# An adaLN-style FFN layer on one core: half-sized moves of h, a seventh two-matmul tile of the second layer, and work re-placed on three engines

## Chip, cores, metric

One core of one Trainium2 chip. The metric is the device time of one execution in microseconds (us); lower is better. The kernel before was run three times.

## What is computed

```python
pooled = conditional_pool(x)          # per batch: tanh(x @ W1 + b1) @ v -> scores; masked softmax; p @ x / count
h  = (pooled - mean) * rsqrt(var + eps) * gamma + beta      # over D = 512
y  = silu(h @ dequant(fc1_q, fc1_scales) + fc1_bias)        # 512 -> 2048
z  = y @ dequant(fc2_q, fc2_scales) + fc2_bias              # 2048 -> 512
out = x + (pooled + 0.5 * z)          # x is (16, 512, 512), float32
```

The scales go with groups of 128 rows of a weight, and the inputs are float32.

## The kernel before, in words

There is no scheduler: each engine has its own program, written out by hand, and semaphores join them. There are 16 batches of 512 rows. `ffn(b, p)` is one batch on each engine, and it has `SLOTS` = 32 slots. In slot i TensorE (PE) does four matmuls of the first layer (`fc1`, L1182 and L1183: two tiles, high and low part of h), then what `PE_PLAN` puts there for a later batch, then half of tile k = i // 2 of the second layer (`fc2`, two of the four banks `z_ps`). First-layer work runs five slots ahead of the second (`fc1_slot`), so slots 27 to 31 already do the first tiles of the next batch, b + 1, and need its h, one 128-column chunk c for each of slots 27 to 30.

`fc2` takes three matmuls for a bank and a tile: y_hi by w_hi (L1210), y_hi by w_lo (L1212), y_lo by w_hi (L1213). The tiles in `WHOLE` (0, 3, 5, 9, 10, 11) keep weights that are exact in the high part, and leave L1212 out; the price is that VectorE (DVE) multiplies each of the four banks in PSUM by a ratio (`rescale_z`, L972) before PE goes on to tile k + 1 in it.

ScalarE (ACT) rescales the first layer's partial sums (`rescale`, L658), applies silu (L652), and casts tile k of y to y_hi (`copy`, L571). VectorE makes y_lo = y_f - y_hi (`split_y`, L963), which `fc2` of tile k waits for.

Around this, `ACT_PLAN`, `DVE_PLAN` and `PE_PLAN` place the pooling of batch b + 1 (and, from slot 28 on, the turning of x for batch b + 2). The piece that matters here is the way of h:

- slots 12 to 15: PE makes the four pooled row blocks (`PZ`), ACT scales them into `scratch` (L632), DVE takes their statistics (`LN`, L899), GpSimd (POOL) adds them to x (`residual`, L493), later the bias (`bias`, L501).
- slot 16: DVE computes the reciprocal deviation (`RSTD`) and normalises the four blocks in place in `scratch` (`H`, L919). That posts `h_ready`.
- the sync engine (SP) then turns h in 32 x 32 blocks: `move_h` issues 16 DMAs from `scratch` to `h_cols` (L442), each 32 partitions by 16 blocks. Before it on SP's queue stand eight loads of turned x for the next but one batch (`load_columns`, L376), behind it eight more. Batches 0 and 1 are turned by PE instead, so 14 batches are moved.
- slot 24 (`DVE_MOVED`): DVE transposes inside the blocks, all four chunks c (`TURNH`, L926), and waits for all 16 DMAs first. ACT applies gamma and beta to each chunk in slots 24 to 27 (`AFFINE`, L642), and DVE splits each into hT_hi and hT_lo in slots 25 to 28 (`SPLITH`, L936 and L938). On ACT the order in a slot is rescale (or silu), then AFFINE, then the copy to y_hi.
- slot 28: DVE turns x of batch b + 2 (`TURN` 0 and 1, L805), ACT copies it (`XT` 0, L571), then casts y_hi of tile 15.

Of the kernel before, what the change touches and what calls it, by code (L numbers as in the profile page):

```python
# [5 lines left out]
ALU = mybir.AluOpType  # L6
# [6 lines left out]
P = 128  # L13
Q = 32
# [4 lines left out]
def build(nc, x, itok, cond_w, cond_b, cond_v, gamma, beta, fc1_q, fc1_s, fc1_b, fc2_q, fc2_s, fc2_b, out):  # L19
    B, S, D = x.shape  # L20
    F = fc1_q.shape[1]
    NJ = S // P
    ND = D // P
    NF = F // P
    UNITS1 = ((0, 2), (2, 3), (3, 4), (4, 6), (6, 8), (8, 10), (10, 12), (12, 16))
    UNITS2 = ((0, 1), (1, 2), (2, 3), (3, 4), (4, 5), (5, 6), (6, 8), (8, 9), (9, 12), (12, 16))
    WHOLE = (0, 3, 5, 9, 10, 11)
    EARLY = 3
    SEGMENTS = ((1, 3, 3), (4, 5, 5), (6, 9, 9))
    NZ = NJ * len(WHOLE)  # L30
    NROWS = 2 * ND + NF + 2 + ND * NF
    NG = NF // ND
# [11 lines left out]
    with ExitStack() as ctx:  # L44
# [3 lines left out]
        def sem(name):  # L48
            return ctx.enter_context(nc.semaphore(name))
# [9 lines left out]
        e1 = [sb(f"e1_{i}", [P, ND, NG * P]) for i in range(2)]  # L59
# [114 lines left out]
        def bank(name):  # L174
# [26 lines left out]
        xt_tr = sem("xt_tr")  # L201
        cols_in = [sem(f"cols_in{s}") for s in range(ND)]
        turned = sem("turned")
        h_moved = sem("h_moved")
        h_turned = sem("h_turned")
        xt_hi = sem("xt_hi")
        xt_ready = sem("xt_ready")
# [64 lines left out]
        ACT_TURN = {24: [("HF", 0)], 25: [("HF", 1)], 26: [("HF", 2)], 27: [("HF", 3)]}  # L272
        DVE_TURN = {25: [("SPLITH", 0)], 26: [("SPLITH", 1)], 27: [("SPLITH", 2)], 28: [("SPLITH", 3)]}
        ACT_MOVED = {24: [("AFFINE", 0)], 25: [("AFFINE", 1)], 26: [("AFFINE", 2)], 27: [("AFFINE", 3)]}
        DVE_MOVED = {24: [("TURNH", 0), ("TURNH", 1), ("TURNH", 2), ("TURNH", 3)], 25: [("SPLITH", 0)], 26: [("SPLITH", 1)],
                     27: [("SPLITH", 2)], 28: [("SPLITH", 3)]}
        DELAY = 4

        PE_FIRST = [("USUM", 0), ("U", 0), ("DSUM", 0), ("PZ", 0), ("PZ", 1), ("PZ", 2), ("PZ", 3)]
        ACT_FIRST = [("XT", 0), ("XT", 1), ("XT", 2), ("XT", 3), ("XSH", 0), ("TANH", 0), ("XSH", 1), ("TANH", 1),  # L280
# [5 lines left out]


        DVE_LATE = {0: [("L2", 1), ("D1", 4)], 1: [("D2", 2)], 2: [("D2", 3)], 3: [("L2", 2), ("D1", 6)], 4: [("D2", 4)],
                    5: [("D2", 5)], 6: [("L2", 4)], 7: [("D1", 8)], 8: [("D2", 6)], 10: [("L2", 6)], 11: [("D1", 10)], 12: [("D2", 8)],
                    14: [("L2", 8)], 15: [("D1", 12)], 16: [("D2", 9)], 19: [("D2", 12)], 22: [("L2", 12)]}  # L290
# [71 lines left out]
        def _(sp):  # L362
# [108 lines left out]
        def _(pool):  # L471
# [17 lines left out]
            assert done[0] == POOL_CONSTS  # L489

            def residual(a, p, J):
                pool.wait_ge(pooled_done, a * NJ + (J + 1))
                nc.gpsimd.tensor_tensor(xt[p][:, J, :], xt[p][:, J, :], pooled[J], ALU.add).then_inc(res_added, 1)  # L493

            def bias(a, p, J):
                pool.wait_ge(res_added, a * NJ + (J + 1))
                if J == 0 and is_first(a):
                    pool.wait_ge(hT_done, ND)
                elif J == 0:
                    pool.wait_ge(h_ready, a * NJ + NJ)  # L500
# [62 lines left out]
        def _(act):  # L563
# [109 lines left out]
            def ffn(b):  # L673
                for i in range(SLOTS):
                    ahead, k, c = fc1_slot(i)
                    if not (ahead and is_last(b)):
                        for t in (k, k + 1):
                            if c < ND - 1:
                                rescale(b + ahead, t, c)
                            else:  # L680
                                silu(b + ahead, t)
                        if c == ND - 1:
                            y_hi_part(b + ahead, k)
                    for ahead, name, n in cond_steps(b, i, ACT_PLAN, ACT_TURN, ACT_MOVED):
                        steps[name](b + ahead, n)
                    if i % 4 == 0:
# [33 lines left out]
        def _(dve):  # L720
# [206 lines left out]

            def split_h(a, c, p=None, ch=None):
# [112 lines left out]
        def _(pe):  # L1041
# [258 lines left out]
```

## Time and profile before

| | us |
|---|---|
| median of 3 runs | 1327.86 (1325.63 to 1328.93) |
| the profiled execution | 1327.16 |
| its span, first to last instruction | 1325.4 |
| busy in the span: PE / DVE / ACT / POOL | 1290.2 / 1069.8 / 1009.2 / 201.5 |

The profile is of one execution. The clock granted to TensorE is 1.00 of full from 60 us on. From one batch's first move of h to the next one's it is about 79 us. A time such as 516.98 is us from the start of the span. Matmuls overlap: a row shows 0.39 for one, but they follow each other at 0.23. Rows on SP are the issuing of a DMA, not its transfer.

### The profile page before, as it was taken

What the parts mean: (1) busy time and instruction counts of PE and PEld (TensorE: products, weight loads), DVE (VectorE), ACT (ScalarE), POOL (GpSimd) and SP (SyncE); (2) the same over time, 40 slices, a digit from 0 to 9 for tenths busy, and PEclk for the clock granted to TensorE, in tenths of its full rate; (3) what the DMA queues carried; (4) which work ended last, traced back from release to release, by engine and by line L of the source; (5) the groups of instructions that cost most, each with busy time, mean ns of one, the idle gap of its engine ahead of it and who ended that gap; (6) DMA issues with size and microseconds to landing.
All of it is one profiled execution on the core that took longest, in us unless ns stands there. A gap on an engine that the chain in (4) does not pass through costs nothing.

```text
span 1325.4 us, 20199 instructions
## 1 busy us (share of the span) xinstructions
PE 1290.2 (97%) x5851; PEld 992.9 (75%) x5851; DVE 1069.8 (81%) x2063; ACT 1009.2 (76%) x1661; POOL 201.5 (15%) x166
## 2 busy tenths in 40 slices
PE   7888999999999999999999999999999999999998
PEld 5665877777777777777777777777777777777787
DVE  6999888888788788888888788888878888888744
ACT  3676777877787887778877788877787877778775
POOL 3302111030301203011030301203021020301100
PEclk7999999999999999999999999999999999999999
DMA  7962103131140322213131230313213031230100
GB/s 226 229 217 32 65 15 66 49 64 65 29 101 1 64 65 49 81 17 66 47 64 66 35 94 1 65 66 57 72 19 80 32 64 65 38 90 1 33 32 32
DMA packets 274235, 84.54 MB, mean 64 GB/s; under 512 B 250026, under 2 KB 250692, under 8 KB 273604
## 3 DMA queue, kind: packets, MB, share of 16 engines
q1 hardware_dynamic: 272944, 82.96, 26.4%
q8 instruction: 64, 1.05, 0.3%
q14 instruction: 55, 0.45, 0.1%
q10 hardware_dynamic: 1172, 0.08, 0.1%
HBM read 51.47 MB, written 16.86 MB: 52 GB/s over the span
## 4 chain that ended last, share of the span: by engine, by line
PE 73%; DVE 13%; ACT 6%; issue 4%; SPq 2%; DMA 1%; ACTq 0%; DVEq 0%
PE y_ps L1182 14%; PE z_ps L1210 14%; PE y_ps L1183 13%; PE z_ps L1213 13%; PE z_ps L1212 8%; SPq L442 2%; DVE scratch L919 2%; ACT y_ps L658 2%; ACT L603 1%; DVE z_ps L972 1%; PE a_ps L1141 1%; PE a_ps L1092 1%; DVE y_lo L963 1%; PE a_ps L1093 1%; PE a_ps L1094 1%
## 5 line engine op out<-in xcount | busy, mean ns | idle before, releaser
L658 ACT ACTIVATE y_ps<-y_ps,ratio 128x512 f32<-128x512 f32 x768 | 474.1, 657 | 153.9 <-PE y_ps L1183 152.1
L1210 PE MATMUL z_ps<-w_hi,y_hi 128*128 128x512 f32 x1024 | 414.0, 404 | 11.4 <-DVE z_ps L972 7.4
L1182 PE MATMUL y_ps<-hT_hi,w 128*128 128x512 f32 x1016 | 409.2, 403 | 7.7 <-ACT y_ps L658 5.3
L1213 PE MATMUL z_ps<-w_hi,y_lo 128*128 128x512 f32 x1024 | 400.8, 391 | 0.0
L1183 PE MATMUL y_ps<-hT_lo,w 128*128 128x512 f32 x1016 | 397.5, 391 | 0.0
L963 DVE TENSOR_TENSOR y_lo<-y_f,y_hi 128x512 fp32r<-128x512 f32 x256 | 198.8, 777 | 146.1 <-ACT y_hi L571 144.9
L1210 PEld LDWEIGHTS z_ps<-w_hi,y_hi 128*128 128x128 f32 x1024 | 192.7, 188 | 84.9 <-issue 25.6
L1182 PEld LDWEIGHTS y_ps<-hT_hi,w 128*128 128x128 f32 x1016 | 191.1, 188 | 86.3 <-ACT y_ps L658 33.4
L1212 PE MATMUL z_ps<-w_lo,y_hi 128*128 128x512 f32 x640 | 249.8, 390 | 0.0
L652 ACT ACTIVATE y_f<-y_ps,vec_cols,mant 128x512 f32<-128x512 f32 x256 | 185.1, 775 | 73.8 <-PE y_ps L1183 73.4
L493 POOL TENSOR_TENSOR x<-x,scratch 128x512 f32<-128x512 f32 x64 | 91.6, 1434 | 941.6 <-ACT scratch L632 941.6
L1213 PEld LDWEIGHTS z_ps<-w_hi,y_lo 128*128 128x128 f32 x1024 | 192.9, 188 | 39.7 <-issue 0.2
L1183 PEld LDWEIGHTS y_ps<-hT_lo,w 128*128 128x128 f32 x1016 | 191.6, 189 | 34.5
L571 ACT ACTIVATE y_hi<-y_f 128x512 fp32r<-128x512 f32 x256 | 160.4, 626 | 1.3 <-PE z_ps L1213 1.3
L1212 PEld LDWEIGHTS z_ps<-w_lo,y_hi 128*128 128x128 f32 x640 | 120.2, 188 | 26.8 <-issue 3.4
L972 DVE TENSOR_TENSOR z_ps<-z_ps,z_ratio 128x512 f32<-128x512 f32 x192 | 122.3, 690 | 0.5
L972 DVE TENSOR_TENSOR z_ps<-z_ps,e 128x512 f32<-128x512 f32 x192 | 119.4, 688 | 0.0
L501 POOL TENSOR_TENSOR x<-x,b2h 128x512 f32<-128x512 f32 x64 | 96.0, 1528 | 82.5 <-DVE scratch L919 73.1
L899 DVE BATCH_NORM_STATS2 stats<-scratch 128x6 f32<-128x512 f32 x64 | 44.0, 688 | 26.4 <-ACT scratch L632 26.4
L632 ACT ACTIVATE scratch<-a_ps,columns 128x512 f32<-128x512 f32 x64 | 44.1, 688 | 22.6 <-DVE columns L891 18.4
L642 ACT ACTIVATE h_rows<-h_rows,vec_cols 128x512 f32<-128x512 f32 x56 | 45.7, 817 | 13.3 <-DVE h_rows L926 13.3
L817 DVE TENSOR_TENSOR xs_lo<-x,xs_hi 128x512 fp32r<-128x512 f32 x60 | 41.6, 693 | 2.1
(207 smaller groups left out, 1166.3 us busy)
## 6 DMA issues: line engine op xcount, KB each, us to landing
x<-in_x_dram SPq DMA_DIRECT2D x64, 256.0 KB, 3.2
out_dram<-x SPq DMA_DIRECT2D x64, 256.0 KB, 2.7
x_cols<-in_x_dram SPq DMA_DIRECT2D x240, 64.0 KB, 2.2
h_cols<-scratch SPq DMA_DIRECT2D x224, 64.0 KB, 2.1
fc_codes<-in_L_ffn_fc_q_dram SPq DMA_DIRECT2D x8, 1024.0 KB, 12.5
fc_scaled<-units_dram SPq DMA_DIRECT2D x4, 1024.0 KB, 17.8
e<-powers_dram SPq DMA_DIRECT2D x3, 1024.0 KB, 15.6
h_rows<-powers_dram SPq DMA_DIRECT2D x1, 1024.0 KB, 10.8
```

Of the source, the lines that this page charges most:

```text
L493: nc.gpsimd.tensor_tensor(xt[p][:, J, :], xt[p][:, J, :], pooled[J], ALU.add).then_inc(res_added, 1)
L501: nc.gpsimd.tensor_tensor(xt[p][:, J, :], xt[p][:, J, :], b2h[:], ALU.add).then_inc(bias_added, 1)
L571: return nc.scalar.activation(o, i, ACT.Copy)
L652: nc.scalar.activation(y_f[k % 2][:], y_ps[k % 2][:], ACT.Silu, bias=b1[:, k:k + 1], scale=mant[:, (ND - 1) * NF + k:(ND - 1) * NF + k + 1 ...
L658: nc.scalar.activation(y_ps[k % 2][:], y_ps[k % 2][:], ACT.Copy, scale=ratio[:, c * NF + k:c * NF + k + 1]).then_inc(scaled, 1)
L963: v.tensor_tensor(y_lo[k % 2][:], y_f[k % 2][:], f32(y_hi[k % 2][:]), ALU.subtract).then_inc(split_done, 1)
L972: v.tensor_tensor(z_ps[r][:], z_ps[r][:], z_ratios[WHOLE.index(k)], ALU.mult).then_inc(z_scaled, 1)
L1182: mm(o, w, hT_hi[:, c, :], start=(c == 0), stop=False, skip_group_check=True)
L1183: last = mm(o, w, hT_lo[:, c, :], start=False, stop=True, skip_group_check=True)
L1210: mm(z_ps[r][:], y_hi[k % 2][:, rows], w2_hi[:, k, :], start=(k == 0), stop=False, skip_group_check=True)
L1212: mm(z_ps[r][:], y_hi[k % 2][:, rows], w2_lo[:, k, :], start=False, stop=False, skip_group_check=True)
L1213: last = mm(z_ps[r][:], y_lo[k % 2][:, rows], w2_hi[:, k, :], start=False, stop=(k == NF - 1 or k in WHOLE), skip_group_check=True)
```

## The change

1. `WHOLE` gets tile 7 (two matmuls for a bank and a tile instead of three, and four more rescales on DVE, in slots 15 and 16).
2. H writes to `normal`, a view of `e1[0]`, a weight-loading buffer that is free by then, laid out as two halves of 256 columns. `move_h` moves each half by itself: 2 x 16 DMAs of 32 partitions by 8 blocks, each half with its own semaphore. TURNH 0 and 1 stay in slot 24 and wait for the first half; TURNH 2 goes to slot 25, behind SPLITH 0, and TURNH 3 to slot 26, behind SPLITH 1; they wait for the second half.
3. POOL's `residual` waits for all of H (h_ready) and H no longer waits for it; `bias` waits for hT_done.
4. The cast of tile 5 to y_hi goes from ACT to DVE (`cast_y`, slot 9); the split of tile 9 goes from slot 17 to slot 16, ahead of H.

```diff
-    UNITS2 = (..., (5, 6), (6, 8), (8, 9), (9, 12), (12, 16))
-    WHOLE = (0, 3, 5, 9, 10, 11)
+    UNITS2 = (..., (5, 6), (6, 7), (7, 8), (8, 9), (9, 12), (12, 16))
+    WHOLE = (0, 3, 5, 7, 9, 10, 11)
...
-        DVE_MOVED = {24: [("TURNH", 0), ("TURNH", 1), ("TURNH", 2), ("TURNH", 3)], 25: [("SPLITH", 0)], 26: [("SPLITH", 1)],
+        DVE_MOVED = {24: [("TURNH", 0), ("TURNH", 1)], 25: [("SPLITH", 0), ("TURNH", 2)], 26: [("SPLITH", 1), ("TURNH", 3)],
                      27: [("SPLITH", 2)], 28: [("SPLITH", 3)]}
+        Y_CAST = 5
+        Y_SOON = 9
+        normal = e1[0][:].rearrange("p j d -> p (j d)").rearrange("p (h j d) -> p h j d", h=2, j=NJ)
...
             def move_h(a):
-                rows = scratch[:, 0:NJ * D].rearrange("p (n d) -> p n d", d=P)
                 sp.wait_ge(h_ready, a * NJ + NJ)
-                for i in range(P // Q):
-                    for j in range(P // Q):
-                        piece = slice(j * Q, (j + 1) * Q)
-                        sp.dma_start(h_cols[piece, :, i * Q:(i + 1) * Q], rows[i * Q:(i + 1) * Q, :, piece]).then_inc(h_moved, 16)
+                for half in range(2):
+                    blocks = slice(half * 2 * NJ, (half + 1) * 2 * NJ)
+                    rows = normal[:, half, :, :].rearrange("p j (c d) -> p (j c) d", d=P)
+                    for i in range(P // Q):
+                        for j in range(P // Q):
+                            piece = slice(j * Q, (j + 1) * Q)
+                            sp.dma_start(h_cols[piece, blocks, i * Q:(i + 1) * Q],
+                                         rows[i * Q:(i + 1) * Q, :, piece]).then_inc(h_moved[half], 16)
...
             def residual(a, p, J):
-                pool.wait_ge(pooled_done, a * NJ + (J + 1))
+                if is_first(a):
+                    pool.wait_ge(pooled_done, J + 1)
+                elif J == 0:
+                    pool.wait_ge(h_ready, a * NJ + NJ)
...
             def turn_h(a, c, p, ch):
-                if c == 0:
-                    dve.wait_ge(h_moved, (a - 1) * 256)
-                chunk = h_cols[:].rearrange("p (j c) n -> p j c n", j=NJ)[:, :, c, :]
+                if c % 2 == 0:
+                    dve.wait_ge(h_moved[c // 2], (a - 1) * 256)
+                chunk = h_cols[:].rearrange("p (h j c) n -> p h j c n", h=2, j=NJ)[:, c // 2, :, c % 2, :]
```

**VectorE, slots 15 and 16 of a batch.** y_lo0 is tile 8, y_lo1 tile 9; L899 and L913 are the statistics of row blocks 2 and 3, L919 and L935 are H. Before:

```order
L963 TENSOR_TENSOR y_lo0<-y_f0,y_hi0 128x512
L899 BN_STATS stats<-scratch 128x6 x2
L903 MEMSET columns4 128x4
...
L919 TENSOR_SCALAR scratch<-scratch,mv,columns4 128x512 x4
L963 TENSOR_TENSOR y_lo1<-y_f1,y_hi1 128x512
```

After:

```order
L979 TENSOR_TENSOR y_lo0<-y_f0,y_hi0 128x512
L993 TENSOR_TENSOR z_ps0<-z_ps0,e1_1 128x512
L993 TENSOR_TENSOR z_ps1<-z_ps1,e1_1 128x512
L913 BN_STATS stats<-scratch 128x6
L993 TENSOR_TENSOR z_ps2<-z_ps2,e1_1 128x512
L993 TENSOR_TENSOR z_ps3<-z_ps3,e1_1 128x512
L913 BN_STATS stats<-scratch 128x6
L917 MEMSET columns4 128x4
...
L979 TENSOR_TENSOR y_lo1<-y_f1,y_hi1 128x512
L935 TENSOR_SCALAR e1_0<-scratch,mv,columns4 128x2x256 x4
```

Four rescales now stand ahead of the last statistics, and y_lo of tile 9 ahead of H.

**The sync engine, one batch, moves of h** (x_cols are the loads of turned x). Before, and after:

```order
L442 DMA h_cols<-scratch 32x16x32 [waits h_ready]
L442 DMA h_cols<-scratch 32x16x32 x15
```

```order
L452 DMA h_cols<-e_0 32x8x32 [waits h_ready]
L452 DMA h_cols<-e_0 32x8x32 x31
```

16 issues of 16 blocks have become 32 issues of 8 blocks.

**VectorE, slots 24 to 28** (L926 and L942 are TURNH; L936/L938 and L952/L954 SPLITH; y_lo1 is tile 13, y_lo0 tile 14). Before:

```order
L926 STREAM_TRANSPOSE h_rows<-h_cols 128x512 x4
L963 TENSOR_TENSOR y_lo1<-y_f1,y_hi1 128x512
L936 CAST hT_hi<-h_rows 128x512
L938 TENSOR_TENSOR hT_lo<-h_rows,hT_hi 128x512
L936 CAST hT_hi<-h_rows 128x512
L938 TENSOR_TENSOR hT_lo<-h_rows,hT_hi 128x512
L963 TENSOR_TENSOR y_lo0<-y_f0,y_hi0 128x512
```

After:

```order
L942 STREAM_TRANSPOSE h_rows<-h_cols 128x512 x2
L979 TENSOR_TENSOR y_lo1<-y_f1,y_hi1 128x512
L952 CAST hT_hi<-h_rows 128x512
L954 TENSOR_TENSOR hT_lo<-h_rows,hT_hi 128x512
L942 STREAM_TRANSPOSE h_rows<-h_cols 128x512
L952 CAST hT_hi<-h_rows 128x512
L954 TENSOR_TENSOR hT_lo<-h_rows,hT_hi 128x512
L942 STREAM_TRANSPOSE h_rows<-h_cols 128x512
L979 TENSOR_TENSOR y_lo0<-y_f0,y_hi0 128x512
```

The transposes of chunks 2 and 3, the first of which waits for the second half, now stand between the two splits and ahead of y_lo of tile 14.

## Rows read from the trace of the kernel before

**Rows 1.** The page: busy time by engine, and the chain's shares by engine.

```profile
PE 1290.2 (97%) x5851; PEld 992.9 (75%) x5851; DVE 1069.8 (81%) x2063; ACT 1009.2 (76%) x1661; POOL 201.5 (15%) x166
...
PE 73%; DVE 13%; ACT 6%; issue 4%; SPq 2%; DMA 1%; ACTq 0%; DVEq 0%
```

**Rows 2.** The chain that ended last, in one batch: start us, us, what.

```profile
515.03 1.93 DVE scratch L919 x4
516.98 0.62 SPq L442
...
528.00 2.08 DMA h_cols<-scratch
530.10 0.72 DVE h_rows L926
531.57 0.61 ACT y_hi L571
532.18 0.55 ACT y_ps L658
532.78 0.49 PE y_ps L1182
...
565.66 0.51 ACT y_hi L571
...
596.61 0.61 DVE y_lo L963
597.27 0.50 PE z_ps L1210
```

**Rows 3.** Timeline, PE: start us, us, engine line, tiles; ten matmuls each apart.

```profile
537.57 0.39 PE L1182 MATMUL y_ps<-hT_hi,w 128*128 128x512 f32 x1
...
539.83 0.39 PE L1182 MATMUL y_ps<-hT_hi,w 128*128 128x512 f32 x1
...
542.10 0.44 PE L1182 MATMUL y_ps<-hT_hi,w 128*128 128x512 f32 x1
```

**Rows 4.** Timeline, VectorE, slots 15 to 28; last bracket: idle before and releaser.

```profile
509.11 0.69 DVE L899 BATCH_NORM_STATS2 stats<-scratch 128x6 f32<-128x512 f32 x1
511.51 0.69 DVE L899 BATCH_NORM_STATS2 stats<-scratch 128x6 f32<-128x512 f32 x1 [1.71 <-ACT scratch L632]
...
520.42 2.48 DVE L972 TENSOR_TENSOR z_ps<-z_ps,e 128x512 f32<-128x512 f32 x4
...
530.10 2.49 DVE L926 STREAM_TRANSPOSE h_rows<-h_cols 128x512 f32<-128x512 f32 x4 [0.19 <-DMA h_cols<-scratch]
...
533.08 0.42 DVE L936 CAST hT_hi<-h_rows 128x512 fp32r<-128x512 f32 x1
...
534.14 0.42 DVE L936 CAST hT_hi<-h_rows 128x512 fp32r<-128x512 f32 x1
...
539.55 1.29 DVE L805 STREAM_TRANSPOSE scratch<-x_cols 128x512 f32<-128x512 f32 x2
```

**Rows 5.** Timeline, SP: the issuing of DMAs.

```profile
8.62 0.59 SPq L410 DMA_DIRECT2D powers_dram<-powers  x1
...
17.40 0.69 SPq L414 DMA_DIRECT2D units_dram<-h_rows  x1
...
115.31 8.29 SPq L376 DMA_DIRECT2D x_cols<-in_x_dram  x16
```

**Rows 6.** Timeline, SP: the moves of h in the batch of rows 2, and the last.

```profile
516.98 11.65 SPq L442 DMA_DIRECT2D h_cols<-scratch  x16
...
1229.54 10.71 SPq L442 DMA_DIRECT2D h_cols<-scratch  x16
```

**Rows 7.** Timeline, ACT, slots 28 and 29.

```profile
540.29 0.63 ACT L571 ACTIVATE part_hi<-scratch 128x512 fp32r<-128x512 f32 x1 [0.71 <-DVE scratch L805]
540.83 0.62 ACT L571 ACTIVATE y_hi<-y_f 128x512 fp32r<-128x512 f32 x1
541.35 1.22 ACT L658 ACTIVATE y_ps<-y_ps,ratio 128x512 f32<-128x512 f32 x2
```

**Rows 8.** Stretches: us, busy (count) PE, PEld, DVE, ACT, POOL, clock, DMA share, GB/s.

```profile
52.00:56.00 4.00, 2.36 (x9) 1.18 (x9) 4.00 (x4) 3.08 (x6) 4.00 (x3) 1.00 0.73 113
56.00:60.00 4.00, 4.00 (x12) 3.13 (x11) 4.00 (x7) 3.01 (x6) 0.34 (x1) 0.57 0.89 209
```

More of the change, by code:

```diff
@@ L25, in build @@
     UNITS1 = ((0, 2), (2, 3), (3, 4), (4, 6), (6, 8), (8, 10), (10, 12), (12, 16))
-    UNITS2 = ((0, 1), (1, 2), (2, 3), (3, 4), (4, 5), (5, 6), (6, 8), (8, 9), (9, 12), (12, 16))
-    WHOLE = (0, 3, 5, 9, 10, 11)
+    UNITS2 = ((0, 1), (1, 2), (2, 3), (3, 4), (4, 5), (5, 6), (6, 7), (7, 8), (8, 9), (9, 12), (12, 16))
+    WHOLE = (0, 3, 5, 7, 9, 10, 11)
     EARLY = 3
-    SEGMENTS = ((1, 3, 3), (4, 5, 5), (6, 9, 9))
+    SEGMENTS = ((1, 3, 3), (4, 5, 5), (6, 7, 7), (8, 9, 9))
     NZ = NJ * len(WHOLE)
@@ L203, in build @@
         turned = sem("turned")
-        h_moved = sem("h_moved")
+        h_moved = [sem(f"h_moved{half}") for half in range(2)]
         h_turned = sem("h_turned")
@@ L274, in build @@
         ACT_MOVED = {24: [("AFFINE", 0)], 25: [("AFFINE", 1)], 26: [("AFFINE", 2)], 27: [("AFFINE", 3)]}
-        DVE_MOVED = {24: [("TURNH", 0), ("TURNH", 1), ("TURNH", 2), ("TURNH", 3)], 25: [("SPLITH", 0)], 26: [("SPLITH", 1)],
+        DVE_MOVED = {24: [("TURNH", 0), ("TURNH", 1)], 25: [("SPLITH", 0), ("TURNH", 2)], 26: [("SPLITH", 1), ("TURNH", 3)],
                      27: [("SPLITH", 2)], 28: [("SPLITH", 3)]}
         DELAY = 4
+        Y_CAST = 5
+        Y_SOON = 9
+        Y_AT = 16
         PE_FIRST = [("USUM", 0), ("U", 0), ("DSUM", 0), ("PZ", 0), ("PZ", 1), ("PZ", 2), ("PZ", 3)]
@@ L288, in build @@
         DVE_LATE = {0: [("L2", 1), ("D1", 4)], 1: [("D2", 2)], 2: [("D2", 3)], 3: [("L2", 2), ("D1", 6)], 4: [("D2", 4)],
-                    5: [("D2", 5)], 6: [("L2", 4)], 7: [("D1", 8)], 8: [("D2", 6)], 10: [("L2", 6)], 11: [("D1", 10)], 12: [("D2", 8)],
+                    5: [("D2", 5)], 6: [("L2", 4)], 7: [("D1", 8)], 8: [("D2", 6)], 9: [("D2", 7)], 10: [("L2", 6)], 11: [("D1", 10)], 12: [("D2", 8)],
                     14: [("L2", 8)], 15: [("D1", 12)], 16: [("D2", 9)], 19: [("D2", 12)], 22: [("L2", 12)]}
@@ L344, in xt_buffers, with by_halves @@
             return first_xt(s) if is_first(a) else (xt_rows[s], hi[:], lo[:])
+        normal = e1[0][:].rearrange("p j d -> p (j d)").rearrange("p (h j d) -> p h j d", h=2, j=NJ)
+        def by_halves(ap):
+            return ap.rearrange("p (h d) -> p h d", h=2)
         def w1_views(k0):
@@ L496, in bias @@
                 pool.wait_ge(res_added, a * NJ + (J + 1))
[L497 to L500, printed above, removed]
+                if J == 0:
+                    pool.wait_ge(hT_done, a * ND + ND)
                 nc.gpsimd.tensor_tensor(xt[p][:, J, :], xt[p][:, J, :], b2h[:], ALU.add).then_inc(bias_added, 1)
@@ L685, in ffn @@
                         steps[name](b + ahead, n)
-                    if i % 4 == 0:
+                    if i % 4 == 0 and i // 2 + 1 != Y_CAST:
                         y_hi_part(b, i // 2 + 1)
@@ L801, in turn_columns @@
             def turn_columns(a, s, p, ch):
-                if s == 0 and by_pe(a - 1):
-                    dve.wait_ge(h_tr, a * ND)
+                if s == 0:
+                    dve.wait_ge(res_added, a * NJ)
+                    if by_pe(a - 1):
+                        dve.wait_ge(h_tr, a * ND)
                 dve.wait_ge(cols_in[s], a * 64)
@@ L917, in normalise @@
                 for J in range(NJ):
-                    dve.wait_ge(res_added, a * NJ + (J + 1))
-                    v.tensor_scalar(pooled[J], pooled[J], mv[:, J, 0:1], rstd[1][:, J:J + 1], ALU.subtract,
+                    if is_first(a):
+                        dve.wait_ge(res_added, J + 1)
+                    o, i = (pooled[J], pooled[J]) if is_first(a) else (normal[:, :, J, :], by_halves(pooled[J]))
+                    v.tensor_scalar(o, i, mv[:, J, 0:1], rstd[1][:, J:J + 1], ALU.subtract,
                                     ALU.mult).then_inc(h_ready, 1)
             def turn_h(a, c, p, ch):
-                if c == 0:
-                    dve.wait_ge(h_moved, (a - 1) * 256)
-                chunk = h_cols[:].rearrange("p (j c) n -> p j c n", j=NJ)[:, :, c, :]
+                if c % 2 == 0:
+                    dve.wait_ge(h_moved[c // 2], (a - 1) * 256)
+                chunk = h_cols[:].rearrange("p (h j c) n -> p h j c n", h=2, j=NJ)[:, c // 2, :, c % 2, :]
                 v.transpose(by_block(h_rows[:, c, :]), chunk).then_inc(h_turned, 1)
@@ L963, in split_y, with cast_y @@
                 v.tensor_tensor(y_lo[k % 2][:], y_f[k % 2][:], f32(y_hi[k % 2][:]), ALU.subtract).then_inc(split_done, 1)
+            def cast_y(b, k):
+                dve.wait_ge(silu_done, b * NF + k + 1)
+                dve.wait_ge(fc2_done, b * NF + (k - 1))
+                v.tensor_copy(y_hi[k % 2][:], y_f[k % 2][:]).then_inc(yhi_done, 1)
             def rescale_z(b, k, r):
@@ L986, in ffn @@
                         split_y(b, (i + 1) // 2)
-                    if i % 4 == 1:
+                    if i % 4 == 1 and (i // 2 + 1 != Y_SOON or is_first(b)):
+                        if i // 2 + 1 == Y_CAST:
+                            cast_y(b, Y_CAST)
                         split_y(b, i // 2 + 1)
@@ L997, in ffn @@
                     for ahead, name, n in cond_steps(b, i, DVE_PLAN_FIRST if is_first(b) else DVE_PLAN, DVE_TURN, DVE_MOVED):
+                        if name == "H" and not is_first(b):
+                            split_y(b, Y_SOON)
                         steps[name](b + ahead, n, p if ahead == 2 else 1 - p, chains[ahead])
+                    if is_last(b) and i == Y_AT:
+                        split_y(b, Y_SOON)
                     if is_first(b):
@@ L1160, in transpose_h @@
                 for J in range(NJ):
-                    last = nc.tensor.transpose(a_ps[c % 2][:, J * P:(J + 1) * P], pooled[J][:, c * P:(c + 1) * P], ident[:])
+                    last = nc.tensor.transpose(a_ps[c % 2][:, J * P:(J + 1) * P], normal[:, c // 2, J, (c % 2) * P:(c % 2 + 1) * P], ident[:])
                 last.then_inc(h_tr, 1)
```

## The prediction

> **What bounds the kernel now.** I read the page first. TensorE is busy for 97% of the span and makes 73% of the chain that ended last; no other engine is busy for more than 81% [rows 1]. So a matmul less is worth its own time, wherever nothing else becomes late. What one is worth is read from the timeline of PE: from 537.57 to 539.83 stand ten matmuls of 512 columns, so one follows another at 0.227 us, and 0.39 is only how long each shows [rows 3]. These ten are also one slot, 2.26 us.
>
> Then I read where the chain leaves PE, and in one batch it does so once at length [rows 2]: H on VectorE ends and releases SP at 516.98, SP issues the 16 moves of h, the last of them is issued at 528.00 and lands 2.08 later, TURNH starts at 530.10, and then AFFINE 0, the cast of tile 13 (531.57) and a rescale (532.18) stand one behind the other on ACT until PE goes on at 532.78. VectorE waited only 0.19 for the landing [rows 4]. So the way of h, 13.1 us from the first issue to TURNH, fits before slot 24 with nothing over. A change to it has to be costed on SP, not on PE.
>
> **Tile 7 with two matmuls.** Four matmuls less in a batch: 4 x 0.227 = 0.91 us, in slots 14 and 15. Four rescales more on VectorE: four in a row take 2.48, 0.60 each from start to start [rows 4]. Two fall in the 1.71 us in which VectorE waited at 511.51. Statistics 2 start at 510.3 instead of 509.11, the third and fourth rescale need PE's last matmul of tile 7 (about 510.9) and end at 512.2, and statistics 3 start there instead of at 511.51: H is 0.7 later. PE does not wait for them, since its tile 8 starts at about 512.
>
> **Tile 9 ahead of H.** y_lo of tile 9 took 0.61 behind H, and PE stood for it: its tile 9 began at 597.27, when that was done [rows 2]. Now it is done before; PE gains some 0.4 at that place, and H is another 0.6 later. Together SP starts its moves at 516.98 + 1.3 = 518.3, while PE is 0.9 to 1.3 ahead of where it was.
>
> **Tile 5 cast by VectorE.** The copy on ACT stood in the chain with 0.51 us [rows 2], which is the upper bound of the gain; nothing is the lower one, if another wait ends last there. I take 0.3.
>
> **The moves.** This is the term that decides. One issue shows 11.65 / 16 = 0.73 us [rows 6]; the last series takes 10.71, which is 0.67 for each, and the 0.94 more of this one lies in a single slow issue; I put one such into each batch. What does an issue of half the blocks take? No row shows one. The issue of 512 pieces of 128 bytes takes 0.67. The two other DMAs that read fewer than 128 partitions of on-chip memory took 0.59 with 64 pieces (64 rows of `powers`) and 0.69 with 1408 (64 partitions x 22) [rows 5]. So from 64 to 1408 pieces the issue grows by 0.1, and 256 pieces should take about 0.61, with the 0.04 between two issues 0.65. The bounds: 0.67, if it does not shrink at all, and 0.34, if it is all in the pieces. The loads of turned x, from HBM, have 512 pieces too and 8.29 / 16 = 0.52 [rows 5]; that is a value between. I take 0.65, since its rows are of the same kind of source.
>
> The Trainium skill (DMA: Bandwidth & Descriptors, Anatomy of one DMA) speaks against the change too: it calls the fixed part of a DMA independent of its size, and says that many descriptors can be emitted before their cost shows. By it alone the issue would keep its 0.67.
>
> *First half*: its 16th issue starts at 518.3 + 15 x 0.65 + 0.9 = 528.95 and lands at 531.0, where 530.1 was. TURNH 0 is 0.9 later than before, while PE comes 0.9 to 1.3 earlier. So the wait on ACT's rescale at 532.78 grows, and PE goes on there at about 533.7.
>
> *Second half*: its last issue starts at 518.3 + 31 x 0.65 + 0.9 = 539.4 and lands at 541.5. TURNH 2 is wanted at about 535. VectorE stands until 541.5, and behind it stand TURNH 2 (0.62), SPLITH 1 (1.06, from one CAST to the next), TURNH 3 (0.62), y_lo of tile 14 (0.61), SPLITH 2 and 3 (2.12) and TURN 0 [rows 4]. PE needs SPLITH 1 in slot 28, at 537.57 before [rows 3]; it comes at 543.2. ACT stands in AFFINE 2 over the same time, with the rescale of slot 27 behind it. TURN 0 starts at 546.5, XT 0 on ACT 0.74 later, and behind XT 0 come the cast of tile 15 (0.54), the rescale of slot 29 (0.52), and PE 0.75 after that rescale's start [rows 3, 7]. That is 549.05 where 542.10 stood: 6.95 later. The gains of tiles 7 and 9 are swallowed by this wait, since what follows hangs on SP; tile 5's 0.3 is kept, as it is ahead of the pooling. Net 6.65 us in each of 14 batches, 93 us.
>
> *TensorE's clock.* PE stands idle for nearly 5 us in slot 27 to 28. In the first 60 us it was busy for 2.36 of 4 us in one stretch, and the granted clock of the next was 0.57, that is mostly 1.2 GHz instead of 2.4 [rows 8]. I expect such a fall in each of the 14 batches. A stretch of 4 us at 0.57 loses 4 x 0.43 = 1.7 us; about 1 us of it lies in the wait for the rescale of slot 29. So 0.7 x 14 = 10 us, between 0 and 24.
>
> The Trainium skill (TensorE: Matmul & The Clock Gate, Part 1) says that activity releases the throttle and idling brings it back; no row in the steady batches shows it yet.
>
> **Pool and the rest.** Residuals and bias of a batch are needed at its end, 80 us later. H lost its wait for POOL, which did not end last (H followed the deviation at once). Turned x of chunk 2 is loaded behind 32 issues instead of 16, lands at about 544 and is wanted at about 550. All three cost nothing. If the moves were quick, their cover would still be there.
>
> **Sum.** Two batches (0 and 15) have no moved h in their slots and gain 0.9 + 0.4 + 0.3 = 1.6 each: -3. Then 93 + 10 - 3 = +100 on the profiled execution's 1327.2 gives 1427 us. The profiled execution is within 1 us of the median of the runs shown.
>
> **Rivals.**
> 1. *Issuing goes with the pieces* (faster). An issue takes 0.34 to 0.38 with its gap. Then the second half lands by 533, before TURNH 2 wants it, nothing waits, and all batches keep their 1.6: 1327.2 - 16 x 1.6 = 1302 us. For it: a load shows 0.52 with just as many pieces, so 0.67 is not a floor. Against it: 64 pieces took 0.59. It decides at 0.44 for an issue: the delay of a batch is 31 x issue - 13.5, which is 6.65 at 0.65 and nothing at 0.44. Chance 0.14. The Trainium skill (DMA: Bandwidth & Descriptors, Bandwidth) calls transfers under 64 KB descriptor-dominated; by that sentence the halves of 32 KB would each cost half, and this rival would be the case.
> 2. *Issues of about 0.52*, as the loads of x. 31 x 0.52 - 13.5 = 2.6 for a batch, 14 x 2.6 - 3 = +34: 1361 us, and up to 1375 with some loss of clock. Chance 0.13.
> 3. *The clock stays low for longer* after each wait, and loses all of 1.7 us or somewhat more: 14 x 1.0 to 2.0 on top of the forecast, 1441 to 1455 us. Chance 0.13.
> 4. *VectorE becomes the bound.* It has 2.4 + 0.4 us more in some 79, of which 65 are busy now; it would be at 87%, so only order matters, which is in the sum. Not given a chance of its own.
>
> **How the numbers follow.** Forecast 0.58, rival 3 0.13, rival 2 0.13, rival 1 0.14, and 0.02 that gains and waits just balance. The time is the forecast's, 1427 us. Its own range is 1405 to 1440 (0.63 and 0.67 for an issue, 0 to 1 us for the clock). The range to hold 8 in 10 goes to rival 2 below and through rival 3 above: 1355 to 1462. A difference of 0.3%, 4 us, is about what a measurement of this kernel tells from no change. Faster by more: 0.14. Within: 0.02. Slower by more: 0.84.
>
> **What would show it.** In the profile after: 32 issues a batch on SP in about 21.5 us, not 11 (wrong if below 15); VectorE idle for 5 to 7 us before a STREAM_TRANSPOSE of h_rows, released by the DMA of h_cols, 14 times; an idle of some 5 us before L1182's matmul in slot 28; about 86 us from batch to batch instead of 79; a granted clock below 1.00 in stretches behind these waits; L1212's line with 576 instead of 640 matmuls. The prediction is wrong if TURNH 2 starts without waiting.

## The result, and the profile after

| | before | after |
|---|---|---|
| median, us | 1328.16 (4 runs) | 1439.0 (4 runs, 1431.55 to 1442.16) |
| ratio | 1 | 1.083, 95% interval 1.0786 to 1.0874 |
| span of the profiled execution | 1325.4 | 1436.5 |
| mean granted clock of TensorE | 0.992 | 0.965 |
| from one batch's first move of h to the next one's | 79.2 | 87.2 |

The change makes the kernel 8.3% slower. The two page lines that answer to [rows 1]:

```profile
PE 1306.2 (91%) x5787; PEld 1000.6 (70%) x5787; DVE 1129.2 (79%) x2144; ACT 1005.6 (70%) x1645; POOL 207.0 (14%) x168
...
PE 46%; SPq 19%; DVE 18%; issue 7%; ACT 7%; DMA 2%; ACTq 0%; DVEq 0%
```

There are 64 matmuls less, and PE makes 46% of the chain instead of 73%; SP, which only issues DMAs, makes 19% instead of 2%. The timeline of SP in one batch, to set beside [rows 6], gives the start in us from the start of the span, the duration in us, and what was issued:

```profile
719.12 4.06 SPq L384 DMA_DIRECT2D x_cols<-in_x_dram  x8
726.99 21.50 SPq L452 DMA_DIRECT2D h_cols<-e  x32
748.68 4.18 SPq L384 DMA_DIRECT2D x_cols<-in_x_dram  x8
```

32 issues take 21.5 us. VectorE in the same batch, for [rows 4]:

```profile
720.93 0.68 DVE L913 BATCH_NORM_STATS2 stats<-scratch 128x6 f32<-128x512 f32 x1
...
739.35 1.30 DVE L942 STREAM_TRANSPOSE h_rows<-h_cols 128x512 f32<-128x512 f32 x2 [1.06 <-DMA h_cols<-e]
741.47 0.69 DVE L979 TENSOR_TENSOR y_lo<-y_f,y_hi 128x512 fp32r<-128x512 f32 x1 [0.81 <-ACT y_hi L583]
742.08 0.42 DVE L952 CAST hT_hi<-h_rows 128x512 fp32r<-128x512 f32 x1
742.53 0.69 DVE L954 TENSOR_TENSOR hT_lo<-h_rows,hT_hi 128x512 fp32r<-128x512 f32 x1
749.81 0.71 DVE L942 STREAM_TRANSPOSE h_rows<-h_cols 128x512 f32<-128x512 f32 x1 [6.59 <-DMA h_cols<-e]
...
756.72 1.39 DVE L979 TENSOR_TENSOR y_lo<-y_f,y_hi 128x512 fp32r<-128x512 f32 x1 [0.63 <-ACT y_hi L583]
758.03 1.78 DVE L824 TENSOR_TENSOR part_lo<-scratch,part_hi 128x512 fp32r<-128x512 f32 x1
```

TURNH 0 waits 1.06 us for the first half, and TURNH 2 then waits 6.59 us for the second. The last two lines are slower than they were: y_lo took 0.69 and part_lo, the low part of a chunk of x, 0.68 at this place before, and POOL adds the bias beside them now. Who waits behind the second half, for the whole span (engine, line, for whom: us in total, times, longest):

```profile
PEld y_ps L1209 <- ACT y_ps L670: 117.9, 76, 5.4
DVE h_rows L942 <- DMA h_cols<-e: 107.4, 28, 6.6
ACT h_rows L654 <- DVE h_rows L942: 104.3, 28, 5.4
```

The wait goes from the DMA to VectorE, from there to ACT's AFFINE, and from the rescale that stands behind it on ACT to PE. 28 waits are two in each of the 14 batches with moved h. PE in the same batch, and then the whole core in stretches of 4 us (columns as in [rows 8]):

```profile
751.97 0.79 PE L1209 MATMUL y_ps<-hT_hi,w 128*128 128x512 f32 x1 [4.99 <-ACT y_ps L670]
...
759.87 0.50 PE L1119 MATMUL a_ps<-part_hi,wc_hi 128*128 128x512 f32 x1
```

```profile
744.00:748.00 4.00, 2.98 (x14) 2.13 (x12) 0.00 (x0) 1.14 (x2) 0.00 (x0) 1.00 0.32 53
748.00:752.00 4.00, 0.03 (x1) 0.03 (x1) 2.15 (x4) 1.44 (x3) 0.00 (x0) 0.69 0.54 86
752.00:756.00 4.00, 4.00 (x10) 3.13 (x11) 3.93 (x8) 3.02 (x5) 0.98 (x1) 0.50 0.42 67
756.00:760.00 4.00, 3.90 (x17) 2.88 (x16) 3.37 (x4) 3.04 (x6) 4.00 (x4) 0.95 0.00 0
```

After 4.99 us of idling the granted clock is 0.50, the lower level of 1.2 GHz, for one stretch, in which PE does 10 matmuls instead of some 18. L1119 is PE's first matmul on the next but one batch's x, and it waits for part_lo.

### The profile page after: what moved, and what is told of

The parts are those of the page before. It is cut to its first block, busy times and chain, and to the rows that moved or that the text cites. A ratio compares the mean times of both kernels' runs of the same rounds, so it can differ in the third digit from the quotient of the medians.

```text
span 1436.5 us, 20429 instructions
## 1 busy us (share of the span) xinstructions
PE 1306.2 (91%) x5787; PEld 1000.6 (70%) x5787; DVE 1129.2 (79%) x2144; ACT 1005.6 (70%) x1645; POOL 207.0 (14%) x168
## 4 chain that ended last, share of the span: by engine, by line
PE 46%; SPq 19%; DVE 18%; issue 7%; ACT 7%; DMA 2%; ACTq 0%; DVEq 0%
SPq L452 19%; PE y_ps L1209 9%; PE z_ps L1237 8%; PE y_ps L1210 8%; PE z_ps L1240 8%; PE z_ps L1239 6%; DVE z_ps L993 3%; DVE y_lo L979 3%; ACT y_ps L670 2%; DVE e L935 2%; DMA h_cols<-e 2%; ACT y_hi L583 2%; DVE stats L913 1%; ACT L615 1%; PE a_ps L1119 1%
## 5 line engine op out<-in xcount | busy, mean ns | idle before, releaser
L1209 PE MATMUL y_ps<-hT_hi,w 128*128 128x512 f32 x1016 | 415.1, 409 | 94.2 <-ACT y_ps L670 89.8
L1237 PE MATMUL z_ps<-w_hi,y_hi 128*128 128x512 f32 x1024 | 421.0, 411 | 15.2 <-DVE z_ps L993 13.0
L1210 PE MATMUL y_ps<-hT_lo,w 128*128 128x512 f32 x1016 | 405.1, 399 | 0.0
L1209 PEld LDWEIGHTS y_ps<-hT_hi,w 128*128 128x128 f32 x1016 | 196.1, 193 | 170.1 <-ACT y_ps L670 117.9
L1239 PE MATMUL z_ps<-w_lo,y_hi 128*128 128x512 f32 x576 | 231.5, 402 | 0.0
L507 POOL TENSOR_TENSOR x<-x,scratch 128x512 f32<-128x512 f32 x64 | 97.6, 1555 | 827.5 <-DVE e L935 817.1
L993 DVE TENSOR_TENSOR z_ps<-z_ps,e 128x512 f32<-128x512 f32 x256 | 160.5, 686 | 0.6
L583 ACT ACTIVATE y_hi<-y_f 128x512 fp32r<-128x512 f32 x240 | 150.2, 626 | 1.3 <-PE z_ps L1240 1.3
L1239 PEld LDWEIGHTS z_ps<-w_lo,y_hi 128*128 128x128 f32 x576 | 112.3, 195 | 26.1 <-issue 3.4
L942 DVE STREAM_TRANSPOSE h_rows<-h_cols 128x512 f32<-128x512 f32 x56 | 38.1, 699 | 107.4 <-DMA h_cols<-e 107.4
L913 DVE BATCH_NORM_STATS2 stats<-scratch 128x6 f32<-128x512 f32 x64 | 43.8, 685 | 2.0 <-ACT scratch L644 2.0
```

The source lines that it names most:

```text
L583: return nc.scalar.activation(o, i, ACT.Copy)
L1209: mm(o, w, hT_hi[:, c, :], start=(c == 0), stop=False, skip_group_check=True)
L1210: last = mm(o, w, hT_lo[:, c, :], start=False, stop=True, skip_group_check=True)
L1237: mm(z_ps[r][:], y_hi[k % 2][:, rows], w2_hi[:, k, :], start=(k == 0), stop=False, skip_group_check=True)
L1239: mm(z_ps[r][:], y_hi[k % 2][:, rows], w2_lo[:, k, :], start=False, stop=False, skip_group_check=True)
```

## The experiments

Theory: one issue on SP costs 0.65 us whatever its size, so the doubled moves bring the second half too late. Rivals for the 111 us: the later H, the rescales of the seventh tile, POOL's moved work, the clock. Times are medians. Each group of runs has its own runs of the kernel before, with medians of 1327.7 to 1328.6, and a ratio is always to those.

**The halves alone, and all but the halves.** The first kernel is the changed one with tile 7, tile 5, tile 9 and POOL put back:

```diff
-    WHOLE = (0, 3, 5, 7, 9, 10, 11)
+    WHOLE = (0, 3, 5, 9, 10, 11)
...
-        Y_CAST = 5
-        Y_SOON = 9
+        Y_CAST = -1
+        Y_SOON = -1
...
+                pool.wait_ge(pooled_done, a * NJ + (J + 1))
...
-                    pool.wait_ge(hT_done, a * ND + ND)
+                    pool.wait_ge(*((hT_done, ND) if is_first(a) else (h_ready, a * NJ + NJ)))
```

The last two places are the waits of `residual` and of `bias`.

> The kernel before with the halved buffer and the 32 half moves alone; tile 7 has three matmuls again, tiles 5 and 9 and POOL's work stand where they stood. Theory (an issue costs 0.65 us whatever its size, and the second half lands late): H is not delayed here, so the second half lands at 516.98 + 31 x 0.65 + 0.9 + 2.1 = 540.1 in the old batch's times, PE's slot 30 starts 7.7 later, at 547.8 instead of 542.1: 5.7 us a batch, 80 in all, and the clock falls as well, 10 to 25 us: 1417 to 1432 us, VectorE waiting 5 us for the DMA of h_cols 14 times. Rival (the loss comes from the delayed H, from tile 7's rescales and from POOL's moved work): 1335 us or less.

Measured: 1419.2 us, ratio 1.0685 (1.0653 to 1.0716), as the theory has it. VectorE waited for the DMA 14 times, 6.3 us each, where 5 were expected:

```profile
DVE h_rows L939 <- DMA h_cols<-e: 88.0, 14, 6.6
```

The second keeps all of the change but makes the moves whole again:

```diff
-                for half in range(2):
-                    blocks = slice(half * 2 * NJ, (half + 1) * 2 * NJ)
-                    rows = normal[:, half, :, :].rearrange("p j (c d) -> p (j c) d", d=P)
+                rows = normal.rearrange("p h j (c d) -> p (h j c) d", d=P)
...
-                if c % 2 == 0:
-                    dve.wait_ge(h_moved[c // 2], (a - 1) * 256)
+                if c == 0:
+                    dve.wait_ge(h_moved[0], (a - 1) * 256)
```

> The changed kernel with one DMA for both halves again: 16 moves of 16 blocks from the new buffer, TURNH 0 waits for all of them; everything else as changed. Theory: the 100 us are the 16 more issues. But H starts its moves 1.3 us later than before, and the landing, not PE, sets slot 26: a batch gains only tile 5's 0.3 and loses 1.3 less what VectorE had to spare, so 1327 + 14 x 1.0 - 3 = 1338 us, between 1325 and 1345, clock 1.00 in the steady batches. Rival (POOL's bias beside the splits, or the seventh rescale, cost much of it): 1370 us or more.

Measured: 1363.8 us, ratio 1.026 (1.0238 to 1.0281). Taking the 16 issues away gives back 75 of the 111 us. But 1363.8 is well above 1338 and outside 1325 to 1345, and closer to the rival's 1370 than to the theory: the rest of the change costs 36 us, where I had 11. Its timeline and waits:

```profile
612.51 11.68 SPq L450 DMA_DIRECT2D h_cols<-e  x16
```

```profile
DVE h_rows L940 <- DMA h_cols<-e: 25.2, 14, 2.8
PEld a_ps L1117 <- DVE part_lo L822: 24.1, 15, 1.8
```

The first wait is the late H (0.7 us in two waits before). The second does not occur before at this line, and leads to POOL.

**POOL's bias.** To the kernel above:

```diff
-                    pool.wait_ge(hT_done, a * ND + ND)
+                    pool.wait_ge(*((hT_done, ND) if is_first(a) else (h_ready, a * NJ + NJ)))
```

> As one_move, and POOL's bias waits for H instead of for the splits, as before. In the changed kernel three SBUF operations of VectorE in slots 29 and 30 took 2.3 us longer while POOL added the bias. Theory (POOL beside VectorE delays the copy that PE waits for): 10 to 20 us faster than one_move. Rival (POOL disturbs VectorE as much at its other place, where y_lo took 1.79 instead of 0.69): no difference beyond 4 us.

Measured: 1351.6 us, 12 faster, as the theory has it. In one_move POOL's four additions stood here:

```profile
635.41 5.93 POOL L511 TENSOR_TENSOR x<-x,b2h 128x512 f32<-128x512 f32 x4 [16.87 <-DVE hT_lo L952]
```

and VectorE beside them:

```profile
637.02 1.48 DVE L977 TENSOR_TENSOR y_lo<-y_f,y_hi 128x512 fp32r<-128x512 f32 x1 [0.63 <-ACT y_hi L581]
638.43 1.76 DVE L822 TENSOR_TENSOR part_lo<-scratch,part_hi 128x512 fp32r<-128x512 f32 x1
640.11 0.70 DVE L817 STREAM_TRANSPOSE scratch<-x_cols 128x512 f32<-128x512 f32 x1
640.74 1.15 DVE L822 TENSOR_TENSOR u_rows<-scratch,coef 128x512 fp32r<-128x512 f32 x1
```

Operations that take 0.65 to 0.69 elsewhere take 1.15 to 1.76, and PE's first projection of the batch after next waits for part_lo.

**The clock.** The changed kernel with work of no use in PE's idle time, in batches 1 to 14:

```diff
+                    if i == 27 and not is_first(b) and not is_last(b):
+                        filler.append(b)
...
+                    if filler:
+                        pe.wait_ge(pooled_done, filler.pop() * NJ + 2 * NJ)
+                        for _ in range(20):
+                            mm(a_ps[0][:], wc_hi[:, 0, :], wc_hi[:].rearrange("p c a -> p (c a)"), start=True, stop=True)
```

> The changed kernel with 20 matmuls of no use (512 columns, 4.5 us) at the end of slot 27 of batches 1 to 14, where PE stands idle for 5.4 us. Theory: the wait stays as long, and the clock does not fall, so the batch loses only the wait: 10 to 25 us faster than the changed kernel, 1414 to 1429, clock 0.99. Rival (the slots behind the wait are bound by VectorE and ACT and not by PE's clock): the clock stays up, and the time is that of the changed kernel within 5 us.

Measured: 1440.0 us against 1439.0, ratio to before 1.0845 (1.0822 to 1.0868). The rival holds: the four runs of the changed kernel spread over 10.6 us, so the two medians fix the difference only to some 6 us, but the 10 to 25 us of the theory are not there. PE filled its time and the clock stayed up:

```profile
744.00 4.70 PE L1265 MATMUL a_ps<-wc_hi 128*128 128x512 f32 x20
749.66 0.50 PE L1209 MATMUL y_ps<-hT_hi,w 128*128 128x512 f32 x1 [0.96 <-ACT y_ps L670]
```

```profile
748.00:752.00 4.00, 3.04 (x14) 1.99 (x13) 3.90 (x9) 3.75 (x6) 0.00 (x0) 1.00 0.73 114
752.00:756.00 4.00, 3.65 (x16) 2.44 (x14) 3.37 (x5) 2.81 (x7) 3.28 (x3) 1.00 0.01 3
```

but what PE gained it then lost waiting for part_lo:

```profile
757.54 0.50 PE L1119 MATMUL a_ps<-part_hi,wc_hi 128*128 128x512 f32 x1 [1.25 <-DVE part_lo L824]
```

For the two slots behind the wait VectorE and ACT set the pace. The traces say this more sharply than the medians: from the start of TURNH 2 to this matmul it is 757.54 - 747.50 = 10.04 us here and 759.87 - 749.81 = 10.06 in the changed kernel; the means of 13 batches are 10.07 and 10.21. So the low clock costs at most some 2 us in all behind the wait. (The rest of a batch is 0.5 us longer in clock_kept, 54.7 for 54.2; why stays open.)

But it costs nothing only because something else is as slow, and that is POOL. In halves_only, where POOL adds the bias elsewhere, PE has the same wait and the same fall of the clock (0.68 in the stretch from 740 to 744), VectorE does part_lo in 0.69, and PE makes 24 matmuls without a gap, at half the pace at first:

```profile
737.24 0.71 DVE L939 STREAM_TRANSPOSE h_rows<-h_cols 128x512 f32<-128x512 f32 x1 [6.51 <-DMA h_cols<-e]
...
744.77 0.69 DVE L821 TENSOR_TENSOR part_lo<-scratch,part_hi 128x512 fp32r<-128x512 f32 x1
```

```profile
739.40 0.79 PE L1202 MATMUL y_ps<-hT_hi,w 128*128 128x512 f32 x1 [4.91 <-ACT y_ps L667]
...
746.45 0.39 PE L1112 MATMUL a_ps<-part_hi,wc_hi 128*128 128x512 f32 x1
```

The 24 matmuls take 7.05 us instead of 24 x 0.227 = 5.45, and PE reaches part_lo 1.0 us after it is done. Over 13 batches part_lo is done 8.20 us behind the start of TURNH 2 (10.03 in the changed kernel), and PE's matmul comes at 9.51. The difference of 1.3 us a batch, up to 18 us in all, is what I estimate the low clock to cost in halves_only; no run keeps the clock up there. In the changed kernel the low clock and POOL's bias lie side by side, and one hides the other.

**Tiles 7 and 9**, each taken out of one_move_bias, and both:

```diff
-    WHOLE = (0, 3, 5, 7, 9, 10, 11)
+    WHOLE = (0, 3, 5, 9, 10, 11)
...
-        Y_SOON = 9
+        Y_SOON = -1
```

The first pair is the edit of base_no7, the second that of base_nosoon, and base_no7_nosoon has both.

> As one_move_bias, and tile 7 has three matmuls again; tile 9 stays ahead of H. Theory: H is 0.6 us late instead of 1.3, and the landing is what counts: 1322 + 14 x 0.6 = 1330 us, that is, taking tile 7's gain of 64 matmuls AWAY makes it about 20 us faster than one_move_bias. Rival (a matmul less is worth its 0.227 us, 14.5 in all): 1366 us.

> As one_move_bias, and tile 9 is split behind H in slot 17 again; tile 7 keeps its two matmuls. Theory: H is 0.7 us late instead of 1.3: 14 x 0.6 = 8 us faster than one_move_bias, 1343. Rival (the wait for y_lo of tile 9, 0.4 us a batch, comes back and counts): 1351 to 1358.

> As one_move_bias (one DMA for both halves, the bias behind H), and tile 7 has three matmuls again and tile 9 is split behind H in slot 17. Left of the change: the new buffer, the cast of tile 5 on VectorE, and the residuals behind H. Theory (one_move_bias is 23 us slower than before since H, and with it the landing that sets slot 26, is 1.3 us later): H is back in its old place, so all 23 go and tile 5's 0.3 a batch stays: 1322 us, between 1315 and 1330. Rival (it is the residuals beside VectorE's y_lo of tile 10, or the cast on VectorE): above 1340.

| tile 7 | tile 9 | median | ratio to before, 95% |
|---|---|---|---|
| two matmuls | ahead of H | 1351.6 | 1.0175 (1.0138 to 1.0212) |
| three | ahead | 1330.2 | 1.0023 (1.0014 to 1.0033) |
| two | behind | 1333.2 | 1.0038 (1.0024 to 1.0052) |
| three | behind | 1324.6 | 0.9978 (0.9967 to 0.9988) |

With 64 matmuls more, tile 7's third ones, the kernel is 21 us faster: with the way of h at its limit, the four rescales ahead of H cost more than the matmuls give. Tile 9 ahead of H costs 5.6 us without tile 7 and 18.4 with it. Counted from PE's first projection of x to the next batch's first move (mean of 13 batches), H is 0.6 us later for tile 9, 0.5 for tile 7 and 1.7 for both: the two delays together are more than their sum. My 8 us for base_nosoon was too small. There VectorE hardly waits for the DMA any more (2.3 us in all), and another wait has come:

```profile
PE z_ps L1231 <- DVE y_lo L977: 23.4, 15, 2.3
```

That is y_lo of tile 9, which the late H now holds up. The last row of the table is the only kernel that beats the one before, by 0.2%: the new buffer, the cast of tile 5, and the residuals behind H. Which of the three does it was not tried. With the bias the 36 us of one_move are accounted for: 12 for the bias, 27 for tiles 7 and 9, less the 3 of the last row.

**How an issue depends on its size**, measured by itself: four quarters of 4 blocks, 64 moves.

> The changed kernel with four quarters instead of two halves: 64 moves of 4 blocks (128 pieces), all awaited by TURNH 0. It measures an issue at a fourth of the size. Theory (an issue hardly depends on its pieces): 0.60 us each and 0.04 between them, a series of 41 us and a little, and 14 x 20 us more than the changed kernel: about 1720 us. Rival (0.5 us or less at 128 pieces, 0.63 at 512 and 0.61 at 256 being a bend): 1620 us or less.

Measured: 1803.6 us in one run. The timeline:

```profile
429.04 41.65 SPq L452 DMA_DIRECT2D h_cols<-e  x64
```

The issue itself took, as the median of all, 0.629 us with 512 pieces (224 issues of the kernel before), 0.611 with 256 (448 of the changed one), 0.601 with 128 (896 here). Doubling the pieces adds about 0.01 or 0.02. The theory has the issue right. It has the time 84 us too low: the series grew by 20.5 us a batch, the batch by 26.1 (113.36 less 87.22). The trace shows where the missing 5.6 us lie. All four chunks wait for the landing here, not only chunks 2 and 3, so PE reaches part_lo 15.98 us behind the landing (the start of TURNH 0, mean of 12 batches) and not 10.21 (of TURNH 2): 5.8 us more.

**Two queues for the moves.** As one_move_bias, with the moves from rows 64 to 127 issued by POOL:

```diff
+                pool.wait_ge(h_ready, a * NJ + NJ)
+                nc.gpsimd.tensor_tensor(poked[:], ones[:, 0:1], ones[:, 0:1], ALU.add)
+                for i in range(2, P // Q):
+                    for j in range(P // Q):
+                        piece = slice(j * Q, (j + 1) * Q)
+                        nc.gpsimd.dma_start(h_cols[piece, :, i * Q:(i + 1) * Q],
+                                            rows[i * Q:(i + 1) * Q, :, piece]).then_inc(h_moved[1], 16)
```

> As one_move_bias, and half of the 16 moves of h are issued by POOL, which is idle then, ahead of its residuals; SP issues 8. Theory (the number of issues one behind the other is what the way of h costs): with POOL's issues at 1.0 us or less the last lands 8 + 2 us behind H instead of 13.1, VectorE never waits for it, PE's wait in slot 26 goes and all gains of tiles 5, 7 and 9 are kept: 1327 - 16 x 1.6 - 14 x 0.7 = 1292 us, between 1285 and 1305. Rival (POOL's issues take 1.5 us or more, or disturb VectorE): 1330 to 1350.

Measured: 1409.6 us, ratio 1.0622 (1.0588 to 1.0657), slower than either theory or rival had it. The moves did what they were to do, eight in 5.15 us on POOL beside eight on SP, and the wait of VectorE for them went. What came instead, POOL and then VectorE:

```profile
542.30 5.15 POOL L521 DMA_DIRECT2D h_cols<-e  x8
547.46 5.01 POOL L506 TENSOR_TENSOR x<-x,scratch 128x512 f32<-128x512 f32 x4
552.44 5.36 POOL L512 TENSOR_TENSOR x<-x,b2h 128x512 f32<-128x512 f32 x4
```

```profile
549.52 7.16 DVE L993 TENSOR_TENSOR y_lo<-y_f,y_hi 128x512 fp32r<-128x512 f32 x1 [0.34 <-ACT y_hi L596]
```

This y_lo took 7.16 us instead of 0.69, while POOL made eight additions without a pause, and each of the 14 batches has one of 6.0 to 7.6. So the residuals went back ahead of H, and tile 9 behind it:

> Two queues for the moves again (8 whole moves on SP, 8 on POOL), with POOL's residuals back ahead of H, as before, so that only the four bias additions follow its moves; tile 7 has two matmuls, tile 5 is cast by VectorE, tile 9 is split in slot 17 as before. In two_queues one y_lo took 7.2 us beside eight additions of POOL in a row. Theory (the way of h bounds the batch, and POOL's eight additions in a row were the only thing that hid it): 1327 - 16 x 1.2 - 14 x 0.7 = 1298 us, between 1288 and 1312. Rival (four additions in a row behind the moves hold up a y_lo just as well): 1340 us or more.

Measured: 1350.8 us, ratio 1.0172 (1.0152 to 1.0192). The rival's number, but mostly not its reason: only three batches have a y_lo of 4.4 to 4.8 us, those in which POOL paused for about 3 us within its eight issues and so came to its additions later, and all have this:

```profile
PE z_ps L1246 <- DVE y_lo L992: 26.3, 15, 2.3
```

Tile 9's y_lo again, behind four rescales and H. Without tile 7:

> As split_issue, with three matmuls for tile 7. Theory (once the way of h no longer bounds the batch, a matmul less is worth its 0.227 us): 64 x 0.227 = 14.5 us slower than split_issue, between 10 and 16. Rival (H's delay by the four rescales still counts): the same or faster, as base_nosoon against base_no7_nosoon, where tile 7 cost 8.6.

Measured: 1335.0 us (1.0051, 1.0032 to 1.007), 16 faster: the rival. And with tiles 7 and 9 both as in the change:

> As split_issue, and tile 9 is split ahead of H, as in the change. In split_issue PE stood 2.1 us in each batch for y_lo of tile 9, which the four rescales of tile 7 push behind a later H. Theory (with a quick way of h, tiles 7 and 9 belong together): that wait goes, 15 x 1.7 to 2.1 us: 1319 to 1326 us, faster than before; the three batches in which a y_lo takes 4.4 to 4.8 us beside POOL stay. Rival (H, later by another 0.6, makes the wait for the way of h come back): 1330 or more.

Measured: 1334.5 us (1.006, 1.004 to 1.008), the rival's side. The wait for y_lo of tile 9 went, as the theory has it, but one y_lo (tile 10) took 2.7 us in 11 batches, where POOL's additions now stand, and ACT's AFFINE waited for VectorE 31.9 us in all. Issuing on two queues takes the way of h off the limit (VectorE waits at most 1.3 us in all for the DMA in the last four kernels), but no kernel tried here turns that into time. Each of them has a y_lo stretched beside POOL's additions; that this alone is what keeps the gain away is not shown, since none was tried without them.

## Why the prediction was right, point by point

- **An issue of half the size takes 0.61 us** [rows 5, 6]: right. It took 0.611, with 0.04 between two, and 32 took 21.50 us where I had about 21.5. The working behind it is thin, two single DMAs of other shapes, and quarters is what confirms that the pieces hardly count. The passage of the Trainium skill that the prediction sets beside it (DMA: Bandwidth & Descriptors, Anatomy of one DMA) says the same of the descriptors, but it describes DMAs that GpSimd issues, and these are issued by SP.
- **H starts 1.3 us later**: right in what it named. Statistics 3 start at 720.93 directly behind the rescales, and y_lo of tile 9 stands ahead of H. Counted from PE's first projection of x (mean of 13 batches), the next first move comes at 54.18 us, where it was 53.15: 1.0 later.
- **First half 0.9 us late, second half 23.2 us behind the first issue**: TURNH 0 started 12.4 us behind it (I had 12.7) and TURNH 2 22.8 us. The wait of 5 to 7 us before TURNH 2 was 6.59.
- **PE idle for nearly 5 us before slot 28**: 4.99, behind ACT's rescale, which stood behind AFFINE 2, as told.
- **The net delay, 6.65 us a batch and 0.7 for the clock**: 8.05 was measured (87.22 less 79.17). Most of the miss lies behind the landing of the second half. From TURNH 2 to the first matmul on part_lo the forecast has 7.55 us to slot 30, 1.1 from there to that matmul as before, and 0.7 for the clock, 9.3 in all; 10.21 was measured, 0.9 more in each of 14 batches. Two terms are behind it:
  - *The clock* falls as forecast, but its price is not 0.7. With POOL's bias where the change puts it, it is 0.1 (10.21 less 10.07, 2 us in all); with the bias elsewhere it would be up to 1.3, by the estimate from halves_only. What a low clock costs is the matmuls it loses less what PE would have waited anyway.
  - *Pool and the rest, all three cost nothing*: wrong for the bias. I asked only when its result is needed, not what runs on VectorE beside it. It brings part_lo 1.8 us later behind TURNH 2 (10.03 for 8.20), and its price is 12 us in one_move, where the clock does not fall.
- **The gains of tiles 7 and 9 are swallowed**: right, and more than that. one_move shows that even with whole moves the rest costs 36 us; I had expected 11. The limit that I read from one wait of 0.19 us [rows 4] holds for H's time as for the number of moves: VectorE waited for the landing in 2 of 14 batches before, so the way of h was just hidden, and nothing later than that is.
- **Rivals**: rivals 1 and 2 needed an issue of 0.38 or 0.52 us; at 0.61 both fall. Rival 3, the longer low clock, was priced at 1441 to 1455, near the result, and is wrong: the clock was low for one stretch, and clock_kept has the same time without it.

The time came out at 1439 for 1427 forecast. The mechanism that was forecast, the second half's landing, is what halves_only shows: 91 us by the halves alone. That this is so near the 93 of the main term is partly luck, since H is not late in halves_only, and an estimated 18 of its 91 us are the clock's, which the forecast counts apart. The costs also do not add up across kernels, 91 by the halves and 36 by the rest against 111 together, at least in part because the clock and the bias hide each other.

## What to carry to other kernels

A series of small DMAs costs its number on the queue that issues them, not its bytes: 64 KB, 32 KB and 16 KB moves took 0.63, 0.61 and 0.60 us to issue. Halving them for an earlier first part delays the last part by as many issues, so ask what the last part is wanted for, and what stands behind the wait on each in-order engine. Where a transfer ends just in time, everything ahead of it on the path (a rescale, a split) costs its full length, and matmuls saved outside that path give nothing. And where an experiment takes one cost away and the time stays, ask what else was hidden behind it: the low clock is free in the changed kernel and, by the estimate above, not in halves_only.

## What the runs showed of the hardware that was not expected

- An operation of VectorE with two inputs in on-chip memory was stretched from 0.69 us to 1.15 to 1.8, 2.7, 4.4 to 4.8, and in every batch of two_queues 6.0 to 7.6 us, while POOL added tiles, with rescales in PSUM beside it at their usual 0.60 from start to start. The Trainium skill (SBUF — State Buffer, Who interferes with whom and Summary: rules for kernel authors) says that such an instruction contends with a GpSimd instruction that reads the same memory and that the second to issue waits for the first. The trace agrees with the contention; but 7.16 us is as long as five of POOL's additions of 1.25 to 1.34, so VectorE waited for more than one of them.
- POOL issued a move of h in 0.65 us (median of 112 in two_queues), nearly as fast as SP with 0.63, but paused for 2.8 to 3.0 us within the series in three of the 14 batches.
- After 5 us without a matmul the clock granted was 1.2 GHz, for about one stretch of 4 us. In the changed kernel at most 2 us were lost by it, since PE was not what the next two slots waited for; in halves_only the same fall put 1.6 us on 24 matmuls in a row, and PE came 1.0 us late to part_lo.
